# Seven block products over the last 32 steps instead of 24, and evictions split in two inside the recurrent chain

## The reference

```python
xW = jnp.einsum('ntd,dg->ntg', x, Wx) + b      # x: 32 x 64 x 256, 4 gates of 256
def step(carry, xw_t):                         # 64 times, one after the other
    prev_h, prev_c = carry
    a = xw_t + prev_h @ Wh
    i, f, o = sigmoid(a[:, :256]), sigmoid(a[:, 256:512]), sigmoid(a[:, 512:768])
    g = jnp.tanh(a[:, 768:])
    next_c = f * prev_c + i * g
    next_h = o * jnp.tanh(next_c)
# hs: 32 x 64 x 256, then a network with weights of +1 and -1 on every step's h:
h = relu(s0 * (concat([hs, -hs]) @ W0)) * 2    # 512 -> 1024
h = relu(s1 * (h @ W1)) * 2                    # 1024 -> 1024
out = x + s2 * (h @ W2)                        # 1024 -> 256
```

## Time and profile before

| what | value |
|---|---|
| median of 3 runs (lowest to highest) | 272.74 us (272.41 to 273.35) |
| the profiled execution's own time | 272.65 us |
| its span, first to last instruction | 270.7 us |
| PE busy | 266.5 us (98%) |
| DVE, ACT, POOL busy | 219.5, 193.0, 48.2 us |
| chain that ended last | PE 97%, DMA 1%, DVE 1% |
| first and last L512 behind step 0 | 22.0 and 220.1 us |
| output DMAs of 128 and of 192 KB, issue to landing | 1.8 and 1.9 us |

### The profile page before, as it was taken

The page is one execution under the profiler, slowest core; times in us unless marked ns, Lnnn a source line. Parts: engine busy times, 40 slices in busy tenths (PEclk is TensorE's granted clock), DMA queues, the critical chain, the costliest instruction groups (busy, mean ns, idle before and its releaser), DMA issues.

```text
span 270.7 us, 9163 instructions
## 1 busy us (share of the span) xinstructions
PE 266.5 (98%) x3568; PEld 220.0 (81%) x3568; DVE 219.5 (81%) x833; ACT 193.0 (71%) x650; POOL 48.2 (18%) x70
## 2 busy tenths in 40 slices
PE   8999999999999999999999999999999999999995
PEld 5877888888999999999999999998887777556663
DVE  3887888888888888888888888888887777998355
ACT  5799898989677768766867677667888976734320
POOL 0010000022211112331222102000222225603030
PEclk9999999999999999999999999999999999999999
DMA  6990000000000000000010001000000010100003
GB/s 208 325 366 2 2 2 0 2 4 2 4 2 1 2 2 22 23 4 4 2 42 0 2 4 42 2 2 2 4 1 2 2 42 0 41 0 0 2 0 116
DMA packets 5434, 8.74 MB, mean 32 GB/s; under 512 B 656, under 2 KB 3472, under 8 KB 5264
## 3 DMA queue, kind: packets, MB, share of 16 engines
q1 hardware_dynamic: 5104, 7.64, 8.1%
q10 hardware_dynamic: 288, 0.52, 0.6%
HBM read 6.07 MB, written 2.10 MB: 30 GB/s over the span
## 4 chain that ended last, share of the span: by engine, by line
PE 97%; DMA 1%; DVE 1%; issue 0%
PE WK L559 36%; PE WK L542 15%; PE G L521 11%; PE WK L577 10%; PE G L512 9%; PE ACC L592 6%; PE G L577 4%; PE WK L612 2%; PE G L542 2%; DMA x<-in_x 1%; DVE x L903 1%; PE G L612 1%; PE ACC L612 1%; PE ACC L542 1%; PE G L559 0%; DVE xs L1012 0%
## 5 line engine op out<-in xcount | busy, mean ns | idle before, releaser
L559 PE MATMUL WK<-h,k 128*128 128x256 f16 (+1 forms) x856 | 107.7, 276 | 0.0
L559 PEld LDWEIGHTS WK<-h,k 128*128 128x128 fp8e5 x856 | 80.8, 98 | 11.2
L717 ACT ACTIVATE tT<-aT 128x64 f32<-128x64 f32 x189 | 51.6, 274 | 42.6 <-DVE aT L965 31.2
L965 DVE TENSOR_REDUCE aT<-G 128x64 f32<-128x128 f32 (+1 forms) x192 | 59.4, 331 | 6.1 <-PE G L521 4.8
L710 ACT ACTIVATE G<-xw 128x256 f32<-128x256 f32 x189 | 52.3, 298 | 0.0
L542 PE MATMUL WK<-xs,wxs 128*128 128x512 f32 x168 | 42.6, 400 | 0.0
L521 PE MATMUL G<-h,w 128*128 128x64 f16 x1008 | 39.5, 192 | 0.0
L512 PEld LDWEIGHTS G<-h,w 128*128 128x128 f16 x1008 | 33.3, 96 | 5.8 <-DVE h L1075 3.1
L542 PEld LDWEIGHTS WK<-xs,wxs 128*128 128x128 f32 x168 | 30.4, 188 | 6.1 <-DVE xs L883 0.3
L512 PE MATMUL G<-h,w 128*128 128x32 f16 x1008 | 35.1, 176 | 0.0
L521 PEld LDWEIGHTS G<-h,w 128*128 128x128 f16 x1008 | 33.2, 97 | 0.0
(11 more groups left out here) (119 smaller groups left out, 287.3 us busy)
## 6 DMA issues: line engine op xcount, KB each, us to landing
x<-in_x SPq DMA_DIRECT2D x3, 512.0 KB, 8.7
out_y<-x SPq DMA_DIRECT2D x10, 128.0 KB, 1.8
xw<-in_wh SPq DMA_DIRECT2D x4, 256.0 KB, 4.9
k<-in_k SPq DMA_DIRECT2D x1, 1024.0 KB, 10.6
out_y<-x SPq DMA_DIRECT2D x4, 192.0 KB, 1.9
x<-in_x ACTq DMA_DIRECT2D x2, 256.0 KB, 3.6
xw<-in_wx SPq DMA_DIRECT2D x4, 128.0 KB, 3.8
xw<-in_wx SPq DMA_DIRECT2D x2, 256.0 KB, 5.1
```

What stands on the lines that cost most here:

```text
L559: ins = eng.matmul(layer_src(tile), w, rhs, start=a == 0, stop=last)
L717: eng.activation(tT[:, B * j0:B * j1], aT[:, j0:j1].rearrange("p j b -> p (j b)"), ACT.Tanh, scale=half_gain0 if t == 0 else half_gain).th ...
L965: eng.tensor_reduce(aT[:, j0:j1], G[g][:, 0:64 * (j1 - j0)].rearrange("p (j h b) -> p j b h", h=2, b=B), op=ALU.add, axis=AX.X).then_inc(a ...
```

## The change

The chunks become 8, 8, 8, 8, 16 and 16 steps (N1 = 4, N2 = 5, `NW` = 512 columns), so the seven products span the last 32 steps. `fill` becomes 2.06 us in every step from 1 on. VectorE's sum of O moves ahead of u. A low part left over from the step before is done inside the next step's chain in two halves of its columns: one between v and c, one between o' and h's high part. Behind the step comes one low part, or two when four or more are queued. Half of chunk N1-1's output tiles move from the tail into the steps' order, and some buffers are laid elsewhere, since 512 columns are wider.

```diff
-CHUNKS = ((0, 8), (8, 8), (16, 8), (24, 8), (32, 8), (40, 12), (52, 12))
-N1, N2 = 5, 6
+CHUNKS = ((0, 8), (8, 8), (16, 8), (24, 8), (32, 16), (48, 16))
+N1, N2 = 4, 5
...
-    return 3.4 if t < 0 else 1.8 if t < 1 else 2.3 if t < 9 else 2.2 if t < 16 else 2.3
+    return 3.4 if t < 0 else 1.8 if t < 1 else 2.06
...
-    return 0.48 if tile[0] == "y" else 0.67 if tile[0] == "x" else 0.95 if tile[:2] == (0, N1) else 0.38
+    return 0.48 if tile[0] == "y" else 0.67 if tile[0] == "x" else 1.3 if tile[:2] == (0, N1) else 0.38 if tile[0] in (0, 1) else 0.67
...
-    return {"mix": 0.65, "y": 0.74, 0: 0.93}[chore[0]]
+    return {"mix": 0.65, "y": 0.74, 0: 1.25}[chore[0]]
...
-        at = (2, 2, 3, 4, 5, 6, 6, 7) if c == 0 else (0, 1, 2, 3, 4, 5, 6, 6) if c < N1 - 1 else (1, 2, 3, 4, 5, 6, 6, 7)
-        return [((0, c + 1, n), 4) for n in range(8) if at[n] == m]
+        at = (2, 2, 3, 4, 5, 6, 6, 7) if c == 0 else (0, 1, 2, 3, 4, 5, 6, 6) if c < N1 - 1 else (3, 4, 5, 6, 7, 7)
+        return [((0, c + 1, n), 4) for n in range(len(at)) if at[n] == m]
...
-    return order + [((f"p{q}", m), 8) for q, m in ((1, 0), (1, 1), (1, 2), (2, 0), (1, 3), (2, 1), (2, 2), (2, 3))]
+    for tile in (("p1", 0), (0, N1, 6), ("p1", 1), (0, N1, 7), ("p1", 2), ("p2", 0), ("p1", 3), ("p2", 1), ("p2", 2), ("p2", 3)):
+        order.append((tile, matmuls(tile)))
+        if tile[0] == "p1" and tile[1] < 2:
+            order += [(("o", N1 - 1, 2 * tile[1] + k), 4) for k in range(2)]
+    return order
...
-    others = outs(N1 - 1, *range(8))
+    others = outs(N1 - 1, *range(4, 8))
...
         late, held = [], []
+        between[t] = [x for x in todo[:1] if x[0] in (0, 1)]
+        todo = todo[len(between[t]):]
+        emptied.update(between[t])
...
-            time = ahead + STEP + spent - CHAIN - KEEP - LOW * (t in W2_STEPS)
-            now = []
-            for x in todo:
-                if len(now) < 2 or sum(map(vector_cost, now + [x])) <= time:
-                    now.append(x)
-            ahead += STEP + spent - max(CHAIN_MIN, CHAIN + sum(map(vector_cost, now)))
-            ahead = min(max(ahead, 0.0), AHEAD)
+            now = todo[:1 if len(todo) + len(late) < 4 or t in W2_STEPS else 2]
...
+            def half_lo(tile, half):
+
+                cols = slice(width(tile) // 2 * half, width(tile) // 2 * (half + 1))
+                e.wait_ge(hi_made[tile[0]], 8 * tile[1] + tile[2] + 1)
+                ins = eng.scalar_tensor_tensor(layer_dst(tile, 1)[:, cols], layer_src(tile)[:, cols], 0.0,
+                                               layer_dst(tile, 0)[:, cols], ALU.max, ALU.subtract)
+                if half == 1:
+                    ins.then_inc(lo_made[tile[0]])
...
                 else:
+                    add_halves(t, O)
                     e.wait_ge(tanhed[F], t + 1)
                     e.wait_ge(c_made, t)
                     eng.scalar_tensor_tensor(uT[:, :], tf, 1.0, cD[:, :], ALU.add, ALU.mult).then_inc(u_made)
-                    add_halves(t, O)
                     e.wait_ge(tanhed[GI], t + 1)
                     eng.scalar_tensor_tensor(vT[:, :], ti, 1.0, tg, ALU.add, ALU.mult).then_inc(v_made)
+                    for tile in between_plan[t]:
+                        half_lo(tile, 0)
                     e.wait_ge(u_made, t)
                     e.wait_ge(v_made, t)
                     eng.scalar_tensor_tensor(cD[:, :], uT[:, :], 0.5, vT[:, :], ALU.mult, ALU.add).then_inc(c_made)
                 e.wait_ge(tanhed[O], t + 1)
                 eng.tensor_scalar(oP[:, :, :].rearrange("p j b -> p (j b)"), to, HS / 2, HS / 2, ALU.mult,
                                   ALU.add).then_inc(o_made)
+                for tile in between_plan[t]:
+                    half_lo(tile, 1)
                 e.wait_ge(c_tanh, t + 1)
```

More of the change, by code:

```diff
@@ L152, in make_plan @@
 def make_plan():
-    pe, act, dve, pool = ([[] for _ in range(T + 2)] for _ in range(4))
+    pe, act, dve, pool, between = ([[] for _ in range(T + 2)] for _ in range(5))
     bank, before = {}, {}
@@ L288, in make_plan @@
             if tile[0] == 0:
-                empty_at[tile] = 1.6 + 2.2 * (tile[2] % 4) + (1.7 if tile[2] < 4 else 3.4)
+                empty_at[tile] = 1.6 + 2.8 * (tile[2] % 4) + (2.1 if tile[2] < 4 else 4.2)
     act[T] = [tile for tile, a in rest if a + 1 == matmuls(tile)]
     dve[T] += [tile for tile in act[T] if tile[0] != "p1"]
-    return pe, act, dve, pool, bank, before
+    return pe, act, dve, pool, between, bank, before
 def lstm_ffn(nc, x_d, small_d, wx_d, wh_d, k0_d, k1_d, k2_d, out_d):
@@ L307, in lstm_ffn @@
         x = sb("x", [P, 2, T * B], F32)
-        xs = sb("xs", [P, 2, 2, 2, 512], F32R)
-        wxs = sb("wxs", [P, 2, 2, NJ, 128], F32R)
+        with nc.sbuf_tensor("xs", [P, 2, 2, 2, 512], F32R) as xs, nc.sbuf_tensor("wxs", [P, 2, 2, NJ, 128], F32R) as wxs:
+            pass
+        t23 = sb("t23", [P, 2, 4, NW], F32)
+        tq01 = sb("tq01", [P, 2, 4, 2, NW], F16)
         small = sb("small", [P, 2 * B + NJ + 3], F32)
@@ L323, in lstm_ffn @@
         seven = sb("seven", [P, 1], U32)
-        h1 = sb("h1", [P, 2, 16 * NW], F16)
+        h1 = sb("h1", [P, 2, 16 * B * CHUNKS[0][1]], F16)
         h2 = sb("h2", [P, 8, 2, NW], F16)
@@ L363, in lstm_ffn @@
         r12 = cut(xflat, 20 * NW, 2, NW)
-        tq = cut(xflat[:, 22 * NW:38 * NW].bitcast(F16), 0, 4, 4, 2, NW)
-        b22 = cut(xflat[:, 38 * NW:42 * NW].bitcast(F16), 0, 4, 2, NW)
+        b22 = cut(xflat[:, 22 * NW:26 * NW].bitcast(F16), 0, 4, 2, NW)
+        tq = [tq01[:, 0], tq01[:, 1], cut(xflat[:, 26 * NW:30 * NW].bitcast(F16), 0, 4, 2, NW), b1[:, 0:4]]
         t4f = cut(w16[:, :].rearrange("p a j k c -> p (a j k c)").bitcast(F32), 0, 4, NW)
@@ L368, in lstm_ffn @@
         qs, d5 = r1[:, 0:4], r12
-        c11, c12 = cut(h1[:, 0], 0, 4, 2, NW), cut(h1[:, 0], 8 * NW, 4, 2, NW)
-        t23 = cut(h1[:, 1].bitcast(F32), 0, 2, 4, NW)
+        c11, c12 = cut(h1[:, 0], 0, 4, 2, NW), cut(h1[:, 1], 0, 4, 2, NW)
         c12f, c22f, c21f = t1f, t23[:, 0], t23[:, 1]
@@ L418, in lstm_ffn @@
         fin_mm, fin_y = ({c: [sem(f"{n}{c}_{mo}") for mo in range(2)] for c in (N1 - 1, N1, N2)} for n in ("fin_mm", "fin_y"))
-        pe_plan, act_plan, dve_plan, pool_plan, bank, before = make_plan()
+        pe_plan, act_plan, dve_plan, pool_plan, between_plan, bank, before = make_plan()
         def layer_dst(tile, part):
@@ L438, in out_sum @@
             return TILE[bank["y", mo]] if c == N2 else (ACC, G[O])[mo] if c == N1 else ACC[:, 256 * mo:256 * mo + 256]
-        factors = {1: (a11, b1[:, 0:4]), 2: (a12, b1[:, 4:8]), 3: (mix[:, 3], b22), 4: (a22, tq[:, 3]),
-                   5: (mix[:, 0], tq[:, 0]), 6: (mix[:, 1], tq[:, 1]), 7: (mix[:, 2], tq[:, 2])}
+        factors = {1: (a11, b1[:, 0:4]), 2: (a12, b1[:, 4:8]), 3: (mix[:, 3], b22), 4: (a22, tq[3]),
+                   5: (mix[:, 0], tq[0]), 6: (mix[:, 1], tq[1]), 7: (mix[:, 2], tq[2])}
         out_parts = {N1: (11, c11, 21, c21), N2: (12, c12, 22, c22)}
@@ L736, in p1_copy @@
                 e.wait_ge(prod_mm[1], tile[1] + 1)
-                e.wait_ge(seeded[O], 32)
+                e.wait_ge(seeded[O], 40)
                 eng.activation(p1s[:, tile[1]], layer_src(tile), ACT.Copy).then_inc(p1_made)
@@ L778, in term_hi @@
                 e.wait_ge(t_made[i], k + 1)
-                eng.activation(tq[:, i, k, 0], term(i, k), ACT.Copy).then_inc(t_hi[i])
+                if i < 2:
+                    e.wait_ge(x_mm, 4 * NJ)
+                elif i == 3:
+                    e.wait_ge(prod_mm[2], 4)
+                eng.activation(tq[i][:, k, 0], term(i, k), ACT.Copy).then_inc(t_hi[i])
             def p5_copy(m):
@@ L925, in term_lo @@
                 e.wait_ge(t_hi[i], k + 1)
-                eng.tensor_tensor(tq[:, i, k, 1], term(i, k), tq[:, i, k, 0], ALU.subtract).then_inc(t_lo[i])
+                eng.tensor_tensor(tq[i][:, k, 1], term(i, k), tq[i][:, k, 0], ALU.subtract).then_inc(t_lo[i])
             def q_sum(m):
```

## The result

| | before | after |
|---|---|---|
| median of 20 runs each (lowest to highest), us | 272.90 (272.41 to 273.47) | 274.06 (273.42 to 274.60) |
| the profiled execution's own time; its span | 272.65; 270.7 | 274.05; 272.3 |
| first L512 (now L514) of step 1 to the end of the last matmul | 245.62 | 246.54 |
| of it, TensorE waiting (below) | 1.18 | 4.28 |
| last matmul's end to the end of the span | 3.02 | 3.30 |

After over before is 1.0042 in the medians, 95% interval 1.0032 to 1.0049: **slower by 0.4%**, 1.16 us. The forecast was 273.1 and "no change" within 0.3%; the range held the time, and the change is just outside "no change". In the experiments three executions fell into a slow state and count in no time: one of a_old_o (441.1 us, granted clock 0.56) and two of b_halves (537.6 and 683.5 us).

A forecast was written before the change was run, and what follows sets the result against it. TensorE's matmul work was taken as the bound. Profiled 272.65 us - 2.1 (work) + 0.2 (end) + 2.3 (waits) = 273.05; with the median 0.09 higher, 273.1 us, called no change; range 270.9 to 275.2.

The forecast's parts named there:

- Part 1: TensorE's matmuls: 192 fewer of 256 columns, 352 widened from 384 to 512; 2.1 us less work.
- Part 2: After the last matmul: one VectorE sum and one DMA grow, together +0.2 us (bounds +0.1 to +0.75).
- Part 3: The recurrence loses its reserve: chain 2.955 us against TensorE's step of 2.93; waits together 2.3 us.
- shortest form: Chain from one h to the next where a step's first matmuls follow h at once: 2.94 us.
- The first rival: The chain holds at 2.94 us, early steps find slack elsewhere: waits 0.9 us or less, about 271.5 us; 30%.
- the rivals of the late c: First half, between v and c, delays c: by 0.05 us, 275.1 us (18%); without overlap by 0.18, 280.7 us (4%).
- One of the prediction's signs: PE no longer busy for 40.00 of 40.00 us in the middle of the kernel.
- (a): Steps 16 to 48: chain of 2.955 us against TensorE's 2.93, in 34 steps; waits of 0.5 us.
- (b): Late steps with 512-column tiles: a step of nine such matmuls waits 0.15 us; 0.7 us in all.
- (c): Early steps: late h and copies on ScalarE, low parts on VectorE, the w2 step; waits of 0.8 us.
- (d): Evictions of p2, 512 columns and never halved, and steps with two low parts behind them; waits of 0.3 us.
- the tail costs nothing more: Tail: VectorE's and ScalarE's pieces grow by a third as TensorE's do; cover shrinks 1.7 us, about 1.3 left.

The follow-up runs named there:

- a_old_o: Changed kernel with VectorE's sum of O back behind u, halves kept: 274.58 us (median of four), 1.0059 of the kernel before.
- b_halves: Kernel before, its chunks, fills and TensorE order kept, with only the new VectorE scheme (sum of O moved, halves): 273.25 us, 1.0009 of the kernel before.
- experiments 1 and 2: Changed kernel without the halves, low parts behind the step again: 277.98 us; changed kernel with both halves between v and c: 278.89 us.
- experiment 10: Kernel before with the new VectorE scheme, fill 2.06 us in steps 1 to 23 and 2.4 later: 275.24 us, 1.0085 of the kernel before.
- b_low24: The run of experiment 10: kernel before with the new VectorE scheme and a lower early fill; 275.24 us.
- Experiment 5: Changed kernel with the two sums of chunk N1-1's output one block earlier in VectorE's tail: 273.8 us (one run).
- c_14: Changed kernel with chunks of 8, 8, 8, 8, 4, 14, 14 steps, fill 2.18 us, tail sums one block earlier, N1-1's output tiles before p2: 274.26 us.
- Experiments 6 and 7: Changed kernel with layer 0's last tiles apart: 274.27 us (one run); that plus tail sums earlier, p2 low part in quarters, w1 in four parts: 274.21 us.
- a_all: The second run of Experiments 6 and 7: changed kernel with four repairs at once; 274.21 us, 1.0041 of the kernel before.

## Where the prediction was right, and the step that failed

**Part 1, columns and matmuls: right.** 2.18 us less work against 2.1. The line through two widths gave 0.216 us for 512 columns; the third products of the tail measure it (timeline of PE):
```profile
230.81 7.07 PE L579 MATMUL WK<-tq,mix 128*128 128x512 f16 x32
...
267.93 1.03 PE L614 MATMUL G<-h,k 128*128 128x512 f16 x4
...
269.00 0.75 DVE L918 SCALAR_TENSOR_TENSOR x<-G,sc,x 128x512 f32<-128x512 f32 x1
```
(7.07 - 1.03) / 28 = 0.216. **Part 2, the end: right** within 0.1: 0.28 against 0.2, the sum 0.75 against 0.62, the landing 2.0 against 1.9, and the rest in between.

**Part 3, the chain: 0.035 us too long.** It is 2.92 where 2.955 was taken. The "shortest form" of 2.94 was not the chain's: L512 started 0.30 behind h there, where a first matmul that waits only for h comes at 0.28, so TensorE held that step up (timeline of PE in the kernel before):
```profile
57.44 0.56 PE L512 MATMUL G<-h,w 128*128 128x32 f16 x16
```
The first rival had the mechanism of the halves right (experiments 1 and 2), though not the time, and the rivals of the late c fell. The halves stand in 30 steps, not in some 45 as those rivals were priced. One of the prediction's signs did not come either: PE is still busy for all of the middle, for the chain leaves it 0.02 us there. Waits (a) were about 0.1 us and not 0.5, outside step 16. (b), nine 512-column matmuls in a late step, was to cost 0.7; the two steps that show it wait 0.09 each (50 and 58), and with step 59 it makes 0.2.

**(c), the early steps: 0.8 against 0.8,** and experiment 10 shows the low fill as their whole cause. Another 0.3 stands in step 16, against 0.1 counted for the weights w2; b_low24 has it too. **(d), p2: 0.43 against 0.3,** in one step, number 61, and there the size was nearer than the mechanism: most of it is the wait for ScalarE's high part, which (d) does not name.

**The step that failed is "the tail costs nothing more"**, and with it the list in (b) to (d), which left out ScalarE's double copies of N1's tiles. The first is 0.58 us, the second 0.63. For the tail I read the third products and the terms in front of them, had 1.3 us left there by my count, and took that for the whole tail. The moved output tiles were also the cover of another wait: the one of L612 (now L614) for the bank that `y_add` reads. The diff shows the cover shrink, in the word `others`; the wait stood in no row that I had picked. Sixteen matmuls at 0.109 are 1.7 us, more than the hole of 0.58, but no run puts them back, so this origin is argued. Experiment 5 shows the wait itself and closes it by one changed constant. For the copies, (c) counted ScalarE's room as 1.0 to 1.1 us and used it for the early steps only; four copies at 0.48 us take 1.9, and by the same rule that step was due to be 0.8 late; it was 0.54 (2.45 against 1.91). It was a term of a kind already in the list, applied to the wrong steps alone.

That 273.1 came within 1 us of the time is in part luck: (a) and (b) were set 0.9 us too high, and that hid most of the 1.2 us of the two terms left out. So the waits were 3.1 us and not 2.3, the end 0.1 more, and the work 0.1 less: 273.05 + 0.8 + 0.1 - 0.1 = 273.85 against a profiled 274.05, in which the start is 0.39 us later and what lies around the span 0.2 less.

**Why a saving of 2.2 us turned into a loss.** Before, TensorE's step was 0.2 us longer than the chain, and each uneven step was paid out of that. The shorter list of matmuls can only help if each step gets shorter; it got all but as short as the chain (2.94 against 2.92). From there every excess of any step is a wait: b_low24 has them with the old matmuls, c_14 (fill 2.18) loses them in the middle, and the changed kernel has 1.64 us more of them at three places behind step 48: ScalarE's wide copies, a p2 tile whose high part comes late, and the tail. Experiments 6 and 7 moved such waits about as much as they removed them (sums of 4.46 and 4.18 against 4.28); only the tail's gain stayed whole. Which order of the last fifteen steps would hold none is open: no run here beat the kernel before.

## What to carry to other kernels

When work is taken from the engine that bounds a kernel, and a chain of small dependent operations runs beside it, compare the two in every step, not in the mean: the gain ends where a step becomes as short as the chain, and the uneven steps (a weight made, a wide copy, two low parts) then cost their full excess. Cutting an operation in halves to fit a gap works to a hundredth of a microsecond if the gap and the half are measured from start to start, and an operation whose input is ready belongs ahead of one that may wait. Before work is moved that served as cover, list every wait behind it on all engines, not only the one that it was put there for.

## What the runs showed of the hardware that was not expected

**VectorE pauses that no wait explains.** Beside the 0.27 us of a_all, there is one of 0.47 us between v's end and c in b_halves and one before o' in the kernel before (timelines of DVE, in this order):
```profile
82.09 0.23 DVE L1077 SCALAR_TENSOR_TENSOR cD<-uT,vT 128x64 f32<-128x64 f32 x1 [0.47 <-DVE vT L1072]
```
```profile
164.94 0.20 DVE L1071 TENSOR_SCALAR oP<-tT 128x64 f32<-128x64 f32 x1 [0.17 <-issue]
```
c usually follows v's end by 0.10. In b_halves the pause cost TensorE 0.21 us; in the kernel before, the reserve of the chain covered it. What causes them the traces don't show.

**Bars are longer than what an operation takes.** On VectorE a 64-column operation has a bar of 0.23 us and the next starts after 0.14 to 0.15; for 128 columns out of PSUM it is 0.28 and 0.20, for 256 columns 0.42 and 0.33. ScalarE's copies of 512 columns have bars of 0.59 and follow one another at 0.48.
